# Local attention: turned queries and keys split in two parts for three-product scores

## The chip, the cores and the metric

The kernel runs on one core of one Trainium2 chip. The metric is the device time of one execution in microseconds (us). Every time below is from the kernel before. A core has five engines with queues of their own: PE (TensorE, matrix products and transposes), DVE (VectorE), ACT (ScalarE), POOL (GpSimd) and SP (which here only issues DMAs). They meet through semaphores alone.

## What is computed

The program computes `x + s * silu(g)`. Here `xn` is the layer norm of `x` (4 sequences of 1024 tokens, 256 wide), `s` is a causal attention over `xn` with 16 heads of 16, and `g` is a two-layer network over `xn` with local attention. The change touches only the local attention, which is, cut to what matters:

```python
for l in range(2):                                   # DEPTH
    q, k, v = split(shift_token(x) @ wqkv[l])        # 8 heads of 64
    q, k = l2norm(q) * q_scale, l2norm(k) * k_scale
    q, k = rotary_xpos(q, k)                         # q*cos*s + rotate_half(q)*sin*s ; k likewise with 1/s
    sim = einsum('bhwid,bhwjd->bhwij', 8 * q, [previous window of k, own window of k])   # windows of 128
    attn = softmax(mask(sim)); o = attn @ [previous v, own v]
    x = x + o @ wo[l]
    x = x + feed_forward(x)
```

## The kernel before

`program` runs five phases one after the other: `phase_project` (causal projections), `phase_causal`, then for each of two layers `phase_window` (local attention) and `phase_feed`, and last `phase_output`. Of them only `phase_window` is changed, so the change is met twice.

`phase_window` works through 32 tiles of 128 tokens; a tile is one window. Tile `w` runs through a software pipeline whose order is written out by hand in one `step` for each engine, called 32 times in a row. A step of tile `w` also does early parts of tiles `w+1` (`a1`), `w+2` (`a2`) and `w+3` (`a3`).

- PE, in a step: `project(w+2)` (18 products of 512 columns: the input in two fp32r parts times the weights in two parts, three products for each); `attend(w)`, that is `turn_p` (16 transposes of the probabilities), `turn_k(w+1)` and `turn_q(w+1)` (4 transposes each), and `values(w)` in four chunks; `turn_h(w+3)`; `score(w+1)` in two halves of four heads; `output(w)` (12 products of 256 columns).
- ACT: 8 `exps`, the copies `copy_q`, `copy_k`, `copy_v` of tile `w+2` out of PSUM, three `copy_p`, `copy_kt(w+1)`, `squares(w+2)`, `copy_qt(w+1)`, `copy_out(w)`, `turned(w+3)`.
- DVE: `normalise` of both halves, `unit(w+1)` (L997: turned values times inverse norms), `copy_last(w)` (L1021), `cosines(w+2)` (L984), `sum_squares(w+2)` (L991), `lo_out(w)` (L1025), `maxima` of the first half of `w+1` (L1007), `lo_of(w+3)` (L976), `maxima` of the second half, `residual(w)` (L1030).
- POOL: waits for both halves of `normalise(w)`, and then computes for tile `w+2` two `sines` (L826), the inverse norms (L832 and the power, L834, which wait for `sum_squares`), and `add` (L840), the sum of cosine and sine parts, which `unit` of the next step reads.

A head has 64 rows, so two heads lie in one 128-row block: `score` (L1181) makes for each of four blocks `c` two products, one on rows 0 to 63 and one on rows 64 to 127, and `score_place` puts them in different PSUM banks. Queries and keys are held as plain f32 (`qt`, `kt`; each score is one f32 product, which the trace shows as two records). The PSUM tile `pX` has four banks that several uses share: `turn_k` writes bank 1 and `turn_q` bank 3, and `turn_h(w+3)` and `project` write these banks again once the copies (`kt_copied`, `qt_copied`) have read them.

"Split" is used in this kernel for making a value v into hi = v rounded to fp32r and lo = v - hi (rounded again), so that a product of two values becomes hi*hi + hi*lo + lo*hi, three products of fp32r. Projections and `output` do this already: ACT writes the hi part, DVE subtracts for the lo part.

Of the kernel before, what the change touches and what calls it, by code (L numbers as in the profile page):

```python
# [731 lines left out]
def score_place(h):  # L732

    return 2 * (h // 4) + h % 2, h // 2 % 2


def phase_window(nc, K, W, F, layer, X, wqkv, wo, qk_scales, w1):

    NW = TILES
    (wo_st, wo_hi, wo_lo, scales, tab, xt, hs, thi, tlo, qk, sq, ss, ssc, rs,  # L740
     tc, tsn, rr, qkn, v, kt, qt, sm, nmax, sums, rsum, pe_, pn, pt, oth, otl, x1, pX, pS) = W.tensors
    qkv_st, qkv_hi, qkv_lo = W.weights
    base, masks = K.base, K.masks
    S = W.sems
# [22 lines left out]
    with nc.Block() as block:  # L767
# [51 lines left out]
        @block.gpsimd  # L819
        def _(pool):  # L820
            def rotated(w, j, it):

                pool.wait_ge(S["k_copied"], ONE + g0 + w + 1)
                pool.wait_ge(S["added"], ONE + g0 + w)
                for z in range(2):
                    pool.tensor_tensor(*sines(w, j, z), ALU.mult).then_inc(S["ts_ready"], 1)  # L826

            def inverse_norm(w, j, it):

                pool.wait_ge(S["ss_ready"], ONE + g0 + w + 1)  # L830
                pool.sem_inc(K.passed, 1)
                pool.tensor_scalar(ssc[:, :], ss[:, j % 2], 1e-24, None, ALU.max).then_inc(S["ssc_ready"], 1)  # L832
                pool.wait_ge(S["ssc_ready"], ONE + g0 + w + 1)
                pool.tensor_tensor(rs[:, j % 2], ssc[:, :], K.mhalf[:, :], ALU.pow).then_inc(S["rs_ready"], 1)  # L834

            def add(w, j, it):
                pool.wait_ge(S["tc_ready"], ONE + g0 + w + 1)
                pool.wait_ge(S["ts_ready"], ONE + 2 * (g0 + w) + 2)
                pool.wait_ge(S["qkn_ready"], ONE + g0 + w)
                pool.tensor_tensor(rr[:, :], tc[:, :], tsn[:, :], ALU.add).then_inc(S["added"], 1)  # L840

            def rope(nxt):
                if nxt:
                    rotated(*nxt)
                    inverse_norm(*nxt)
                    add(*nxt)


            pool.memset(kt[:, :, 1], 0.0).then_inc(S["cleared"], 1)
            pool.memset(v[:, 3], 0.0).then_inc(S["cleared"], 1)  # L850
            pool.wait_ge(S["w_loaded"], ONE + (layer + 1) * 2 * 16)
            pool.tensor_tensor(tab[:, :].rearrange("p t f d -> p t (f d)"), base[:, :].rearrange("p t f d -> p t (f d)"),
                               scales[:, :, :].rearrange("p f d -> p (f d)")[:, None, :]
                               .broadcast_to([P, TPB, 4 * LD]), ALU.mult).then_inc(S["tab_ready"], 1)
            pool.wait_ge(S["tab_ready"], ONE + layer + 1)
            inverse_norm(0, 0, 0)
            rope((1, 1, 0))

            pool.wait_ge(S["w_split"], ONE + 4 * layer + 4)
            pool.sem_inc(K.passed, 1)  # L860
            pool.memset(qkv_st[:, :, TAIL_COL:TAIL_COL + P], 0.0).then_inc(F.sems["cleared"], 1)

            def step(w, j, it):
                nxt = ahead(w, j, it, 2)
                if nxt:
                    pool.wait_ge(S["pn_ready"], ONE + 2 * (g0 + w) + 2)
                rope(nxt)

            steps(pool, step)

        @block.scalar
        def _(act):
# [50 lines left out]
                act.activation(qt[:, :, :], pX[:, 3].rearrange("p (c t) -> p c t", c=4), ACT.Copy)\  # L923
                   .then_inc(S["qt_copied"], 1)

            act.wait_ge(S["cleared"], ONE + 2 * layer + 2)
            turned(0, 0, 0)
            for z in range(3):
                act.wait_ge(S["qkv_loaded"][z], ONE + (layer + 1) * 16)
# [16 lines left out]
            def step(w, j, it):  # L946
                a1, a2, a3 = (ahead(w, j, it, n) for n in (1, 2, 3))
                exps(w, j, it, 0)
                exps(w, j, it, 1)
                if a2:  # L950
                    copy_q(*a2)
                    copy_k(*a2)
                    copy_v(*a2)
                for ch in range(3):
                    copy_p(w, j, it, ch)
                if a1:
                    copy_kt(*a1)
# [11 lines left out]
        def _(dve):  # L969
# [24 lines left out]
            def unit(w, j, it):  # L994
                dve.wait_ge(S["added"], ONE + g0 + w + 1)
                dve.wait_ge(S["rs_ready"], ONE + g0 + w + 1)
                dve.tensor_tensor(qkn[:, :].rearrange("p (h d) -> p h d", d=LD),  # L997
                                  rr[:, :].rearrange("p (h d) -> p h d", d=LD),
                                  rs[:, j % 2][:, :, None].broadcast_to([P, 2 * LH, LD]), ALU.mult)\
                   .then_inc(S["qkn_ready"], 1)  # L1000

            def maxima(w, t, hf):

# [41 lines left out]
            dve.tensor_tensor(rr[:, :], tc[:, :], tsn[:, :], ALU.add).then_inc(S["added"], 1)  # L1045
            split(3, wo_lo[:, :, :], wo_st[:, :, :], wo_hi[:, :, :])
            unit(0, 0, 0)
            cosines(1, 1, 0)
            sum_squares(1, 1, 0)
            maxima(0, 0, 0)  # L1050
# [3 lines left out]
            def step(w, j, it, t):  # L1054
# [2 lines left out]
                normalise(w, j, it, 1)  # L1057
                if a1:
                    unit(*a1)
                copy_last(w, j, it)  # L1060
                if a2:
                    cosines(*a2)
                    sum_squares(*a2)
                lo_out(w, j, it)
                if a1:
# [11 lines left out]
        def _(pe):  # L1077
            def turn_h(w, j, it):
                pe.wait_ge(S["x_loaded"][j], ONE + (layer * (NW // 4) + it + 1) * 32)
                pe.wait_ge(S["qt_copied"], ONE + g0 + w)  # L1080
                pe.wait_ge(S["t_lo"], ONE + g0 + w)
                pe.transpose(pX[:, 3, 0:P], xt[:, j, 0:P], K.ident[:, :])
                pe.transpose(pX[:, 3, P:D], hs[:, j], K.ident[:, :]).then_inc(S["t_ready"], 1)

            def project(w, j, it):
                pe.wait_ge(S["t_lo"], ONE + g0 + w + 1)
                for z in range(3):
                    if z == 0:
                        pe.wait_ge(S["kt_copied"], ONE + g0 + w)
                        pe.wait_ge(S["q_copied"], ONE + g0 + w)  # L1090
                    elif z == 1:
                        pe.wait_ge(S["ot_lo"], ONE + g0 + w)
                        pe.wait_ge(S["k_copied"], ONE + g0 + w)
                    else:
                        pe.wait_ge(S["qt_copied"], ONE + g0 + w)
                        pe.wait_ge(S["v_copied"], ONE + g0 + w)
                        if isinstance(w, int) and w == 0:
                            pe.wait_ge(S["t_lo"], ONE + g0 + 2)
# [32 lines left out]
            def attend(w, j, it):  # L1131
# [2 lines left out]
                pe.wait_ge(S["x1_ready"], ONE + 2 + g0 + w)  # L1134
                turn_p(w, j, it, 0, 0)
                pe.wait_ge(S["q_copied"], ONE + g0 + last)
                pe.wait_ge(S["kt_copied"], ONE + 1 + g0 + w + 1)
                turn_p(w, j, it, 1, 1)
                pe.wait_ge(S["v_copied"], ONE + g0 + last)
                pe.wait_ge(S["qt_copied"], ONE + 1 + g0 + w + 1)  # L1140
                turn_p(w, j, it, 2, 3)
                pe.wait_ge(S["pt_first"], ONE + 3 * (g0 + w) + 1)
                turn_p(w, j, it, 3, 0)
# [36 lines left out]

            def score(w, j, it, hf):  # L1181
                if hf == 0:
                    pe.wait_ge(S["kt_copied"], ONE + 1 + g0 + w + 1)
                    pe.wait_ge(S["qt_copied"], ONE + 1 + g0 + w + 1)
                if not isinstance(w, int) or w > 0:
                    pe.wait_ge(S["max_ready"], ONE + 2 * (g0 + w) + hf - 1)
                for c in (2 * hf, 2 * hf + 1):
                    for r in range(2):
                        rows = slice(r * LD, (r + 1) * LD)
                        bank, slot = score_place(2 * c + r)  # L1190
                        ins = pe.matmul(pS[:, bank, slot], qt[rows, c, :], kt[rows, c].rearrange("p s t -> p (s t)"),  # L1191
                                        start=True, stop=True)
                ins.then_inc(S["s_ready"], 1)

            for w in range(2):
                turn_h(w, w, 0)
            for w in range(2):
                project(w, w, 0)
            pe.wait_ge(S["cleared"], ONE + 2 * layer + 2)
            turn_k(0, 0, 0)  # L1200
            turn_q(0, 0, 0)
            score(0, 0, 0, 0)
# [522 lines left out]
def window_tensors(nc, c, W):  # L1725
# [8 lines left out]
        sb("ss", [P, 2, 2 * LH], F32), sb("ssc", [P, 2 * LH], F32), sb("rs", [P, 2, 2 * LH], F32),  # L1734
        sb("tc", [P, 2 * INNER], F32), sb("tsn", [P, 2 * INNER], F32), sb("rr", [P, 2 * INNER], F32),
        sb("qkn", [P, 2 * INNER], F32),
        sb("v", [P, 4, INNER], F32), sb("kt", [P, KI, 2, P], F32), sb("qt", [P, KI, P], F32),
        sb("sm", [P, LH, 2 * P], F32), sb("nmax", [P, LH], F32), sb("sums", [P, LH], F32), sb("rsum", [P, LH], F32),
        sb("pe", [P, LH, 2 * P], F32), sb("pn", [P, LH, 2 * P], F32), sb("pt", [P, 4, 512], F32),
        sb("oth", [P, INNER], F32R), sb("otl", [P, INNER], F32R), sb("x1", [P, 2, D], F32),  # L1740
# [19 lines left out]
def program(nc, x, wqk, wv, woc, wqkv, wo, qk_scales, ln_g, ln_b, w1, b1, w2, b2, tables, out):  # L1760

    with ExitStack() as c:
# [16 lines left out]
            "w_loaded", "w_hi", "w_split", "cleared", "tab_ready", "x1_ready", "ss_ready", "k_copied", "sq_ready",  # L1779
            "added", "ts_ready", "ssc_ready", "rs_ready", "rsum_ready", "pn_ready", "t_ready", "t_hi", "t_lo",  # L1780
            "q_ready", "k_ready", "v_ready", "q_copied", "v_copied", "max_ready", "exp_done", "pt_ready",
            "pt_first", "pt_last", "kt_ready", "kt_copied", "qt_ready", "qt_copied", "ot_ready", "ot_hi", "ot_lo",
            "tc_ready", "qkn_ready", "s_ready", "wo_ready"), {"qkv_loaded": 3, "x_loaded": 4, "x1_stored": 2})
        FS = semaphores(c, nc, "f_", (
            "w_loaded", "w1_loaded", "ln_loaded", "w_hi", "w_split", "cleared", "x2_ready", "hn_ready", "xb_ready", "mv_ready", "ve_ready",
# [2 lines left out]


        K.starts = [(x, ONE) for sems in (WS, FS) for v in sems.values() for x in (v if isinstance(v, list) else [v])]  # L1790
        K.starts += [(WS["kt_copied"], 1), (WS["exp_done"], 2), (WS["x1_ready"], 2), (WS["ot_lo"], 2),
                     (WS["qt_copied"], 1), (FS["act_ready"], 2), (FS["x2_ready"], 2)]
        made = c.enter_context(nc.semaphore("made"))
        K.zeroed = zeroed = c.enter_context(nc.semaphore("zeroed"))
        with nc.Block() as block:
# [86 lines left out]
```

## Time and profile before

| | |
|---|---|
| time, median of 3 runs | 2072.05 us (2068.73 to 2073.27) |
| the profiled execution, its own time | 2068.08 us |
| its span in the trace | 2066.3 us |
| PE busy | 1863.8 us (90%) |
| DVE busy | 1521.2 us (74%) |
| ACT busy | 1206.2 us (58%) |
| POOL busy | 955.0 us (46%) |
| PE in the score products, L1191 | 132.2 us summed durations, x1024 records, mean 398 ns with mutual overlap |

Busy is the time in which at least one of an engine's instructions runs. An instruction's record on DVE or ACT also covers its start-up and drain, so that the next record can begin some 0.08 us before it ends, and it covers time in which the instruction is held up after it began. Matmul records overlap much more; their pace is read from start to start.

### The profile page before, as it was taken

The page shows a single profiled execution, that of the slowest core. Times are in us where ns is not written, and L with a number is a line of the kernel's source. Part 1 is how long each engine was busy: PE and PEld are TensorE (multiplying, and loading weights), DVE is VectorE, ACT ScalarE, POOL GpSimd, SP SyncE. Part 2 cuts the span into 40 slices and gives each one's busy share as a digit, 9 for nine tenths or more (in the row PEclk, how much of TensorE's full clock was granted, in tenths as well). Part 3 has the DMA queues.
Part 4 walks back from the last instruction along what each step waited for, and adds up shares of the span by engine and source line. Part 5 has one row for each costly group of instructions (what it writes and reads, how often), then busy time and mean ns, then how long its engine had stood idle before and what let it go on. Part 6 is the DMA issues. An engine that isn't in the chain of part 4 may idle for free. (4 is left out here: it accounts for less than half of the span.)

```text
span 2066.3 us, 41715 instructions
## 1 busy us (share of the span) xinstructions
PE 1863.8 (90%) x12960; PEld 1337.3 (65%) x12960; DVE 1521.2 (74%) x4128; ACT 1206.2 (58%) x2501; POOL 955.0 (46%) x797
## 2 busy tenths in 40 slices
PE   5879999999996999999986999689999999699975
PEld 4733333333332788888875888578888887588875
DVE  5667888888872899999985554289999998555424
ACT  3414666666665677777774343267777777443323
POOL 3442122222222777777752333267777776233310
PEclk9868999999998999999998999899999999899988
DMA  5792456446512000000022221200000002211237
GB/s 199 240 185 39 63 75 81 63 65 83 70 21 67 14 26 26 27 27 26 26 66 61 57 58 49 80 14 26 26 26 26 26 26 66 64 34 58 62 119 242
DMA packets 150662, 134.67 MB, mean 65 GB/s; under 512 B 31298, under 2 KB 133118, under 8 KB 150398
## 3 DMA queue, kind: packets, MB, share of 16 engines
q1 hardware_dynamic: 149182, 131.75, 27.4%
q10 hardware_dynamic: 1344, 1.31, 0.2%
q8 instruction: 60, 0.98, 0.2%
q14 instruction: 76, 0.62, 0.1%
HBM read 86.60 MB, written 46.16 MB: 64 GB/s over the span
## 5 line engine op out<-in xcount | busy, mean ns | idle before, releaser
L636 ACT ACTIVATE ca_pr<-ca_pS 128x1024 f32<-128x1024 f32 (+3 forms) x384 | 296.5, 811 | 209.7 <-PE ca_pS L550 169.2
L895 ACT ACTIVATE w_pe<-w_sm,w_nmax 128x256 f32<-128x256 f32 x512 | 253.4, 497 | 140.7 <-DVE w_nmax L1007 140.7
L826 POOL TENSOR_TENSOR w_tsn<-w_qk,w_tab 128x512 f32<-128x512 f32 x124 | 251.0, 2045 | 163.0 <-DVE w_pn L1016 163.0
L470 POOL TENSOR_SCALAR_AFFINE_SELECT ca_pr<-ca_pr 128x256 f32<-128x256 f32 x256 | 103.8, 409 | 386.7 <-ACT ca_pr L636 382.2
L662 DVE CUSTOM_DVE_ANT_0 ca_masked<-ca_pR,ca_later 128x256 f32<-128x256 f32 (+3 forms) x512 | 235.6, 485 | 41.1 <-PE ca_pR L526 38.0
L526 PE MATMUL ca_pR<-ca_ks,ca_qs 96*128 96x512 bf16 (+3 forms) x768 | 220.3, 345 | 16.6 <-DVEq L719 13.2
L1007 DVE CUSTOM_DVE_ANT_0 w_sm<-w_pS,masks 128x256 f32<-128x256 f32 x512 | 185.7, 420 | 21.2 <-PE w_pS L1191 21.1
L666 DVE TENSOR_REDUCE ca_mx<-ca_pR 128x1 f32<-128x512 f32 x256 | 175.6, 686 | 29.0 <-PE ca_pR L526 27.2
L550 PE MATMUL ca_pS<-ca_qs,ca_ks 98*128 98x512 bf16 (+3 forms) x768 | 183.7, 330 | 8.7 <-issue 3.5
L834 POOL TENSOR_TENSOR w_rs<-w_ssc,mhalf 128x16 f32<-128x16 f32 x64 | 187.9, 2935 | 5.3
L1016 DVE TENSOR_SCALAR w_pn<-w_pe,w_rsum 128x256 f32<-128x256 f32 x512 | 186.9, 427 | 4.5
L526 PEld LDWEIGHTS ca_pR<-ca_ks,ca_qs 96*128 96x128 bf16 x768 | 70.5, 97 | 172.3 <-DVE ca_mx L662 89.6
L571 PE MATMUL ca_pO<-ca_pr,ca_va 128*32 128x512 f32 (+3 forms) x1536 | 164.2, 499 | 1.9 <-POOL ca_pr L470 1.1
L1104 PE MATMUL w_pX<-big_hi,w_thi 128*128 128x512 f32 x384 | 153.3, 399 | 9.8 <-DVE big_lo L972 9.8
L1327 POOL TENSOR_TENSOR f_alo<-f_af,f_ahi 128x512 fp32r<-128x512 f32 x80 | 105.7, 1326 | 116.9 <-ACT f_ahi L1379 116.9
L1104 PE MATMUL w_pX<-big_hi,w_tlo 128*128 128x512 f32 x384 | 151.9, 396 | 0.0
L1104 PE MATMUL w_pX<-big_lo,w_thi 128*128 128x512 f32 x384 | 151.7, 395 | 0.0
L1512 PE MATMUL f_pH<-f_thi,big_hi 128*128 128x512 f32 x352 | 142.9, 406 | 9.2 <-DVE f_tlo L1415 8.3
L840 POOL TENSOR_TENSOR w_rr<-w_tc,w_tsn 128x1024 f32<-128x1024 f32 x62 | 149.0, 2402 | 0.0
L1113 PE MATMUL w_pX<-ident,w_pn 128*128 128x128 f32 x1024 | 133.4, 280 | 15.2 <-DVE w_pn L1016 15.1
L1512 PE MATMUL f_pH<-f_tlo,big_hi 128*128 128x512 f32 x352 | 140.8, 400 | 0.0
L1512 PE MATMUL f_pH<-f_thi,big_lo 128*128 128x512 f32 x352 | 140.5, 399 | 0.0
(166 smaller groups left out, 4423.0 us busy)
## 6 DMA issues: line engine op xcount, KB each, us to landing
QKP<-p_parts SPq DMA_DIRECT2D x32, 384.0 KB, 2.9
ca_qs<-QKP SPq DMA_DIRECT2D x96, 128.0 KB, 6.8
ca_ks<-QKP SPq DMA_DIRECT2D x96, 128.0 KB, 7.2
w_xt<-X SPq DMA_DIRECT2D x64, 128.0 KB, 2.0
X<-w_x SPq DMA_DIRECT2D x64, 128.0 KB, 1.7
f_hh<-X SPq DMA_DIRECT2D x32, 256.0 KB, 4.9
f_xr<-X SPq DMA_DIRECT2D x16, 512.0 KB, 4.9
X<-f_x SPq DMA_DIRECT2D x16, 512.0 KB, 3.3
```

Of the source, the lines that this page charges most:

```text
L526: pe.matmul(bank[:, 0:w], qs[0:SHIFT_ROW, u, h, i * P:(i + 1) * P], ks[0:SHIFT_ROW, u, h, k0:k0 + w], start=True, stop=True).then_inc(ring ...
L550: ins = pe.matmul(pS[:, pair, hh, 0:w], ks[:, u, h, j * P:(j + 1) * P], qs[:, u, h, q0:q0 + w], start=True, stop=True)
L636: act.activation(pr[:, k % 2, pair, :, 0:w], pS[:, pair, :, 0:w], ACT.Exp, scale=CS).then_inc(p_ready, 1)
L662: dve.tensor_tensor_reduce(masked[:, jb % RING, 0:w], pR[jb % RING][:, 0:w], later[:, 512 - w:512], -1.0, BIG, ALU.add, ALU.min, mx[:, i, ...
L666: dve.tensor_reduce(mx[:, i, h, ch:ch + 1], pR[jb % RING][:, 0:w], AX.X, ALU.max, negate=True).then_inc(ring_free, 1)
L826: pool.tensor_tensor(*sines(w, j, z), ALU.mult).then_inc(S["ts_ready"], 1)
L834: pool.tensor_tensor(rs[:, j % 2], ssc[:, :], K.mhalf[:, :], ALU.pow).then_inc(S["rs_ready"], 1)
L895: ins = act.activation(pe_[:, h], sm[:, n], ACT.Exp, bias=nmax[:, n:n + 1], scale=-1.0, accum_out=sums[:, h:h + 1])
L1007: ins = dve.tensor_tensor_reduce(sm[:, n], pS[:, n // 2, n % 2], masks[:, 0 if t == 0 else 1 + t % 2], -1.0, BIG, ALU.add, ALU.min, nmax[: ...
L1016: ins = dve.tensor_scalar(pn[:, h], pe_[:, h], rsum[:, h:h + 1], None, ALU.mult)
L1104: ins = pe.matmul(pX[:, 1 + z], t[:, j % 2, k], m[:, k, cols], start=i == 0, stop=i == len(terms) - 1)
L1512: ins = pe.matmul(pH[:, ch % 2, half], m[:, k, cols], t[:, j, k], start=i == 0, stop=i == len(terms) - 1)
```

## The change

Turned queries and keys are now kept as fp32r hi parts (`qt`, `kt`) and lo parts (`qtl`, `ktl`). ACT's copies write the hi parts. Two new DVE instructions, `lo_k` and `lo_q`, make the lo parts out of the same PSUM banks. `score` makes three fp32r products for each head instead of one f32 product. The inverse norms are computed as before. On DVE the order of a step changes: `cosines(w+2)` comes ahead of `copy_last(w)`, and `lo_k(w+1)` and `lo_q(w+1)` stand between `copy_last(w)` and `sum_squares(w+2)`. On ACT `copy_qt(w+1)` comes ahead of `squares(w+2)`. On PE all waits for `kt_copied` and `qt_copied` become waits for `kt_lo` and `qt_lo`. POOL clears `ktl`'s first half too.

```diff
@@ pool, before the steps
-            pool.memset(kt[:, :, 1], 0.0).then_inc(S["cleared"], 1)
+            pool.memset(kt[:, :, 1].bitcast(F32), 0.0).then_inc(S["cleared"], 1)
+            pool.memset(ktl[:, :, 1].bitcast(F32), 0.0).then_inc(S["cleared"], 1)
@@ act step
                 if a1:
                     copy_kt(*a1)
+                    copy_qt(*a1)
                 if a2:
                     squares(*a2)
-                if a1:
-                    copy_qt(*a1)
@@ dve
+            def lo_k(w, j, it):
+                dve.wait_ge(S["kt_copied"], ONE + g0 + w + 1)
+                dve.tensor_tensor(ktl[:, :, j % 2], pX[:, 1].rearrange("p (c t) -> p c t", c=4),
+                                  kt[:, :, j % 2].bitcast(F32), ALU.subtract).then_inc(S["kt_lo"], 1)
+            def lo_q(w, j, it):
+                dve.wait_ge(S["qt_copied"], ONE + g0 + w + 1)
+                dve.tensor_tensor(qtl[:, :, :], pX[:, 3].rearrange("p (c t) -> p c t", c=4),
+                                  qt[:, :, :].bitcast(F32), ALU.subtract).then_inc(S["qt_lo"], 1)
@@ dve, before the steps
             unit(0, 0, 0)
+            lo_k(0, 0, 0)
+            lo_q(0, 0, 0)
             cosines(1, 1, 0)
@@ dve step
                 if a1:
                     unit(*a1)
-                copy_last(w, j, it)
                 if a2:
                     cosines(*a2)
+                copy_last(w, j, it)
+                if a1:
+                    lo_k(*a1)
+                    lo_q(*a1)
+                if a2:
                     sum_squares(*a2)
                 lo_out(w, j, it)
@@ pe, in turn_h, project, attend and score: each wait of this kind
-                pe.wait_ge(S["kt_copied"], ...)
-                pe.wait_ge(S["qt_copied"], ...)
+                pe.wait_ge(S["kt_lo"], ...)
+                pe.wait_ge(S["qt_lo"], ...)
@@ pe, score
                 for c in (2 * hf, 2 * hf + 1):
-                    for r in range(2):
-                        rows = slice(r * LD, (r + 1) * LD)
-                        bank, slot = score_place(2 * c + r)
-                        ins = pe.matmul(pS[:, bank, slot], qt[rows, c, :], kt[rows, c].rearrange("p s t -> p (s t)"),
-                                        start=True, stop=True)
+                    for i, (q, k) in enumerate(((qt, kt), (qt, ktl), (qtl, kt))):
+                        for r in range(2):
+                            rows = slice(r * LD, (r + 1) * LD)
+                            bank, slot = score_place(2 * c + r)
+                            ins = pe.matmul(pS[:, bank, slot], q[rows, c, :],
+                                            k[rows, c].rearrange("p s t -> p (s t)"), start=i == 0, stop=i == 2)
@@ window_tensors
-        sb("kt", [P, KI, 2, P], F32), sb("qt", [P, KI, P], F32),
+        sb("kt", [P, KI, 2, P], F32R), sb("ktl", [P, KI, 2, P], F32R),
+        sb("qt", [P, KI, P], F32R), sb("qtl", [P, KI, P], F32R),
```

## Rows read from the trace of the kernel before

**Rows 1.** Engines' busy time in a layer's window steps, in us.

```profile
core 0: us, PE busy (x) PEld busy (x) DVE busy (x) ACT busy (x) POOL busy (x), PEclk, DMA share, GB/s
683.00:1072.00 389.00, 384.70 (x3123) 323.66 (x3122) 358.60 (x1004) 299.28 (x819) 289.50 (x152) 1.00 0.10 31
```

**Rows 2.** Timeline of DVE: start us, us, instruction. `unit` of tiles 2 and 30.

```profile
700.93 1.22 DVE L997 TENSOR_TENSOR w_qkn<-w_rr,w_rs 128x1024 f32<-128x1024 f32 x1
...
1059.77 1.22 DVE L997 TENSOR_TENSOR w_qkn<-w_rr,w_rs 128x1024 f32<-128x1024 f32 x1
```

**Rows 3.** Timeline of PE in one period, merged where alike.

```profile
910.46 2.00 PE L1191 MATMUL w_pS<-w_kt,w_qt 64*128 64x256 f32 x16
912.38 0.39 PE L1177 MATMUL w_pX<-w_wo_hi,w_oth 128*128 128x256 f32 x1
912.61 0.28 PE L1177 MATMUL w_pX<-w_wo_lo,w_oth 128*128 128x256 f32 x1
912.73 0.28 PE L1177 MATMUL w_pX<-w_wo_hi,w_oth 128*128 128x256 f32 x1
```

**Rows 4.** Timeline of PE, window of 0.3 us at the first two score records.

```profile
910.46 0.49 PE L1191 MATMUL w_pS<-w_kt,w_qt 64*128 64x256 f32 x2
```

**Rows 5.** Timeline of DVE in the same period.

```profile
904.61 0.18 DVE L1013 RECIPROCAL w_rsum<-w_sums 128x4 f32<-128x4 f32 x1
...
905.88 1.22 DVE L997 TENSOR_TENSOR w_qkn<-w_rr,w_rs 128x1024 f32<-128x1024 f32 x1
907.32 0.69 DVE L1021 COPY w_pt<-w_pX 128x512 f32<-128x512 f32 x1 [0.22 <-PE w_pX L1113]
907.93 1.39 DVE L984 TENSOR_TENSOR w_tc<-w_qk,w_tab 128x1024 f32<-128x1024 f32 x1
909.44 1.22 DVE L991 TENSOR_REDUCE w_ss<-w_sq 128x16 f32<-128x1024 f32 x1
910.84 0.69 DVE L1025 TENSOR_TENSOR w_otl<-w_pX,w_oth 128x512 fp32r<-128x512 f32 x1 [0.17 <-ACT w_oth L905]
911.80 0.42 DVE L1007 CUSTOM_DVE_ANT_0 w_sm<-w_pS,masks 128x256 f32<-128x256 f32 x1 [0.27 <-PE w_pS L1191]
...
915.63 1.81 DVE L1016 TENSOR_SCALAR w_pn<-w_pe,w_rsum 128x256 f32<-128x256 f32 x4
917.38 0.18 DVE L1013 RECIPROCAL w_rsum<-w_sums 128x4 f32<-128x4 f32 x1
```

**Rows 6.** Timeline of POOL in the same period.

```profile
906.40 1.83 POOL L826 TENSOR_TENSOR w_tsn<-w_qk,w_tab 128x512 f32<-128x512 f32 x1 [2.67 <-DVE w_pn L1016]
908.20 2.29 POOL L826 TENSOR_TENSOR w_tsn<-w_qk,w_tab 128x512 f32<-128x512 f32 x1
910.86 0.25 POOL L832 TENSOR_SCALAR w_ssc<-w_ss 128x16 f32<-128x16 f32 x1 [0.38 <-DVE w_ss L991]
911.20 2.92 POOL L834 TENSOR_TENSOR w_rs<-w_ssc,mhalf 128x16 f32<-128x16 f32 x1
914.09 2.40 POOL L840 TENSOR_TENSOR w_rr<-w_tc,w_tsn 128x1024 f32<-128x1024 f32 x1
```

**Rows 7.** Timeline of ACT in the same period.

```profile
908.36 1.05 ACT L915 ACTIVATE w_sq<-w_qk 128x1024 f32<-128x1024 f32 x1
909.30 0.59 ACT L923 ACTIVATE w_qt<-w_pX 128x512 f32<-128x512 f32 x1
...
913.30 0.51 ACT L895 ACTIVATE w_pe<-w_sm,w_nmax 128x256 f32<-128x256 f32 x1 [2.22 <-DVE w_nmax L1007]
...
917.25 0.58 ACT L884 ACTIVATE w_qk<-w_pX 128x512 f32<-128x512 f32 x1
```

**Rows 8.** Timeline of DVE at the start of layer 1's window phase.

```profile
672.31 2.21 DVE L997 TENSOR_TENSOR w_qkn<-w_rr,w_rs 128x1024 f32<-128x1024 f32 x1 [0.49 <-POOL w_rs L834]
674.44 2.30 DVE L984 TENSOR_TENSOR w_tc<-w_qk,w_tab 128x1024 f32<-128x1024 f32 x1
```

**Rows 9.** Timeline of POOL at the same place.

```profile
672.18 1.26 POOL L826 TENSOR_TENSOR w_tsn<-w_qk,w_tab 128x512 f32<-128x512 f32 x1
673.40 2.26 POOL L826 TENSOR_TENSOR w_tsn<-w_qk,w_tab 128x512 f32<-128x512 f32 x1
```

More of the change, by code:

```diff
@@ L740, in phase_window @@
     (wo_st, wo_hi, wo_lo, scales, tab, xt, hs, thi, tlo, qk, sq, ss, ssc, rs,
-     tc, tsn, rr, qkn, v, kt, qt, sm, nmax, sums, rsum, pe_, pn, pt, oth, otl, x1, pX, pS) = W.tensors
+     tc, tsn, rr, qkn, v, kt, ktl, qt, qtl, sm, nmax, sums, rsum, pe_, pn, pt, oth, otl, x1, pX, pS) = W.tensors
     qkv_st, qkv_hi, qkv_lo = W.weights
@@ L924, in copy_qt @@
                    .then_inc(S["qt_copied"], 1)
-            act.wait_ge(S["cleared"], ONE + 2 * layer + 2)
+            act.wait_ge(S["cleared"], ONE + 3 * layer + 3)
             turned(0, 0, 0)
@@ L1079, in turn_h @@
                 pe.wait_ge(S["x_loaded"][j], ONE + (layer * (NW // 4) + it + 1) * 32)
-                pe.wait_ge(S["qt_copied"], ONE + g0 + w)
+                pe.wait_ge(S["qt_lo"], ONE + g0 + w)
                 pe.wait_ge(S["t_lo"], ONE + g0 + w)
@@ L1088, in project @@
                     if z == 0:
-                        pe.wait_ge(S["kt_copied"], ONE + g0 + w)
+                        pe.wait_ge(S["kt_lo"], ONE + g0 + w)
                         pe.wait_ge(S["q_copied"], ONE + g0 + w)
@@ L1094, in project @@
                     else:
-                        pe.wait_ge(S["qt_copied"], ONE + g0 + w)
+                        pe.wait_ge(S["qt_lo"], ONE + g0 + w)
                         pe.wait_ge(S["v_copied"], ONE + g0 + w)
@@ L1136, in attend @@
                 pe.wait_ge(S["q_copied"], ONE + g0 + last)
-                pe.wait_ge(S["kt_copied"], ONE + 1 + g0 + w + 1)
+                pe.wait_ge(S["kt_lo"], ONE + 1 + g0 + w + 1)
                 turn_p(w, j, it, 1, 1)
                 pe.wait_ge(S["v_copied"], ONE + g0 + last)
-                pe.wait_ge(S["qt_copied"], ONE + 1 + g0 + w + 1)
+                pe.wait_ge(S["qt_lo"], ONE + 1 + g0 + w + 1)
                 turn_p(w, j, it, 2, 3)
@@ L1182, in score @@
                 if hf == 0:
-                    pe.wait_ge(S["kt_copied"], ONE + 1 + g0 + w + 1)
-                    pe.wait_ge(S["qt_copied"], ONE + 1 + g0 + w + 1)
+                    pe.wait_ge(S["kt_lo"], ONE + 1 + g0 + w + 1)
+                    pe.wait_ge(S["qt_lo"], ONE + 1 + g0 + w + 1)
                 if not isinstance(w, int) or w > 0:
@@ L1198, in _ @@
                 project(w, w, 0)
-            pe.wait_ge(S["cleared"], ONE + 2 * layer + 2)
+            pe.wait_ge(S["cleared"], ONE + 3 * layer + 3)
             turn_k(0, 0, 0)
@@ L1736, in window_tensors @@
         sb("qkn", [P, 2 * INNER], F32),
-        sb("v", [P, 4, INNER], F32), sb("kt", [P, KI, 2, P], F32), sb("qt", [P, KI, P], F32),
+        sb("v", [P, 4, INNER], F32), sb("kt", [P, KI, 2, P], F32R), sb("ktl", [P, KI, 2, P], F32R),
+        sb("qt", [P, KI, P], F32R), sb("qtl", [P, KI, P], F32R),
         sb("sm", [P, LH, 2 * P], F32), sb("nmax", [P, LH], F32), sb("sums", [P, LH], F32), sb("rsum", [P, LH], F32),
@@ L1781, in program @@
             "q_ready", "k_ready", "v_ready", "q_copied", "v_copied", "max_ready", "exp_done", "pt_ready",
-            "pt_first", "pt_last", "kt_ready", "kt_copied", "qt_ready", "qt_copied", "ot_ready", "ot_hi", "ot_lo",
+            "pt_first", "pt_last", "kt_ready", "kt_copied", "kt_lo", "qt_ready", "qt_copied", "qt_lo", "ot_ready", "ot_hi", "ot_lo",
             "tc_ready", "qkn_ready", "s_ready", "wo_ready"), {"qkv_loaded": 3, "x_loaded": 4, "x1_stored": 2})
@@ L1790, in program @@
         K.starts = [(x, ONE) for sems in (WS, FS) for v in sems.values() for x in (v if isinstance(v, list) else [v])]
-        K.starts += [(WS["kt_copied"], 1), (WS["exp_done"], 2), (WS["x1_ready"], 2), (WS["ot_lo"], 2),
-                     (WS["qt_copied"], 1), (FS["act_ready"], 2), (FS["x2_ready"], 2)]
+        K.starts += [(WS["kt_lo"], 1), (WS["exp_done"], 2), (WS["x1_ready"], 2), (WS["ot_lo"], 2),
+                     (WS["qt_lo"], 1), (FS["act_ready"], 2), (FS["x2_ready"], 2)]
         made = c.enter_context(nc.semaphore("made"))
```

## The prediction

> **What bounds the kernel now.** The changed code runs only in the window phases, so I read those alone: first the busy time by stretch, then one period engine by engine.
>
> The stretch view [rows 1] shows PE busy for 384.7 of 389 us at full granted clock, DVE for 358.6, ACT 299.3, POOL 289.5. PE looks like the bound, and DVE is not far off. One tile takes one period: from a reciprocal to the same one a tile later is 917.38 - 904.61 = 12.77 us [rows 5]. Over 28 tiles, `unit` to `unit`, it is (1059.77 - 700.93) / 28 = 12.82 [rows 2]; some steps have a little loop overhead.
>
> A busy share does not show loops, and there is one that passes through POOL and DVE. I follow it in [rows 5, 6]:
> - `sum_squares` ends at 910.66 (909.44 + 1.22). POOL starts L832 at 910.86, the power at 911.20, `add` at 914.09, and ends it at 916.49.
> - DVE's first normalising group (L1016) began at 915.63 and takes 1.81 for four, while 905.88 - 904.61 is only 1.27 for a reciprocal and four of them. It sat blocked until POOL's `add` let go, and the next reciprocal is at 917.38.
> - Reciprocal to `unit` is 1.27. `unit` runs 1.22.
> - POOL's first `sines` is recorded from 906.40 but takes 1.83 and ends at 908.23, and the second 2.29. An undisturbed one took 1.26 [rows 9]. The first waited for `unit` to end (907.10), the second for `cosines`.
> - `cosines` starts at 907.93, at once behind `copy_last`, and takes 1.39 against 1.22 for `unit`, which is as large: it waits for the first `sines` and ends at 909.32. `sum_squares` follows at 909.44.
>
> Along this loop there is 0.20 us between `sum_squares` and L832, a hand-over, and 0.12 ahead of `sum_squares`; nothing else is free. It closes in 12.77 by itself. So the kernel has two bounds of nearly one length: PE's order, and this loop. In the present order `copy_last` costs the loop nothing, because it lies in the time in which POOL's first `sines` holds the port.
>
> **The change part by part, per tile.**
>
> Scores on PE. Now they take 912.38 - 910.46 = 1.92, for 8 f32 products, 16 records [rows 3]. The two row halves run side by side: two records that last together 0.49, with a mean of 398 ns for one on this line [rows 4]. The new form has 24 fp32r products of 256 columns. The nearest row is `output`, fp32r with 256 columns, one per 0.12 (912.73 - 912.61) [rows 3]. If halves still run side by side that is 12 x 0.12 = 1.44 and some ramp, a gain of 0.3 to 0.48. If they don't, it is 24 x 0.12 = 2.88, a loss of 0.96, and PE's order takes 13.73. I take the first, since the same halves do it in f32; as the sum turns out, even the second stays under the new loop.
>
> The Trainium skill (TensorE: Matmul & The Clock Gate, section LDWEIGHTS) prices a weight load by its columns, however few rows: about 107 ns for 128. As an estimate from that page, 24 loads in series would be 2.57 us, more than today's scores. The trace has no fp32r load on half the rows; for f32 it shows both halves going together.
>
> DVE's two subtractions. They read PSUM and SBUF and write 128x512 fp32r, exactly the form of `lo_out`, 0.69 [rows 5]. Such an instruction advances the queue by 0.61 (`copy_last` to `cosines`, 907.93 - 907.32). So 1.22 more DVE work per tile, in front of `sum_squares`, that is inside the loop.
>
> `cosines` moved ahead of `copy_last`. This takes `copy_last` out of its cover. The question is who gets the port when `unit` ends: POOL's `sines`, pending since 906.40, or `cosines`, next in DVE's queue. The start of the phase has just that order, `unit` then `cosines` with `sines` pending: `cosines` is recorded 674.44 with 2.30, nearly twice its length, and the pending `sines` 673.40 with 2.26, ending 675.66 [rows 8, 9]. `unit` ended 674.52; `sines` took the next 1.14, `cosines` only then. POOL won. So in the new step `cosines` still ends at 909.32, as before, and `copy_last` comes behind it.
>
> Then, in this period's time: `copy_last` 909.24, `lo_k` 909.85, `lo_q` 910.46, `sum_squares` 911.07 instead of 909.44: 1.63 later (0.61 x 3 - 0.20 for waits that go). The rest of the loop is unchanged: L832, the power and `add` follow `sum_squares` at fixed distance, and the next reciprocal follows `add`. The period becomes 12.77 + 1.63 = 14.40.
>
> Does anything end later still? `score` now waits for `lo_q`, done at 911.15, against a start of 910.46 now. `turn_h` (0.4) comes between, so scores start at some 911.6 and the first half is ready near 912.7; `maxima` follows `lo_out`, which ends 912.9, so it starts at 912.8 instead of 911.80 [rows 5]. The exponentials start 1.5 later and fill 3.95 (913.30 to 917.25) [rows 7], which ends them at 918.3; the reciprocal of the second half is due at 904.61 + 14.40 = 919.0. Hidden by 0.7. With serial scores `maxima` would start 0.7 later, and it just ties. PE stops before `values`' last chunk for `copy_last` (about 0.4) and before `turn_h` for `lo_q`; its work of 12.3 to 13.7 fits in 14.40. If the loop were not the cover, these waits would cost up to 1.
>
> ACT's exchange (`copy_qt` before `squares`): squares end near 909.92 instead of 909.41 (908.36 + 1.05) [rows 7], hidden behind 911.07. The added memset is some 0.5 us while loads are on their way: nothing, 0.5 per layer at most.
>
> The sum. From 12.82 to 14.40 is 1.58 a tile. 31 steps in each of two layers have a next tile: 62 x 1.58 = 98 us. First and last tiles have other orders (`cosines(1)` waits for the two subtractions; the last two steps have no `cosines`); I leave them at the same price, give or take 6. On the profiled execution's 2068.08 (span 2066.3 and 1.8 around it) this gives 2166. The median of the runs shown is 4 above that execution, 0.2%, which is also about what a measurement can tell from no change; half of it added, the forecast is 2168 us. Its own range is 2150 to 2185.
>
> The Trainium skill (SBUF — State Buffer, section SBUF: two separate sides) says that VectorE and GpSimd share a port pair as an exclusive lock, taken by an instruction with two SBUF inputs too, held by whichever starts first while the other fully blocks. The rows of `unit`, `cosines` and `sines` agree (2.30 against 1.22). It does not say who is next when both wait; read as VectorE going straight on, it would give rival A.
>
> **The rivals.**
>
> A: VectorE keeps the port. `cosines` runs 907.02 to 908.24, `copy_last` and the low parts follow, and `sum_squares` then waits for ACT's squares at 909.97 or so, 0.53 later than now. Period 13.30, 62 x 0.48 = 30, about 2100. For it: the two are back to back in one queue. Against: both rows at the phase's start. 13%.
>
> B: faster. The loop is no bound, and PE's order remains one; the subtractions lie in DVE's idle 30 us, and PE's gain of 0.3 to 0.48 is paid out 62 times, about 25 us: 2047. It decides in my favour or not at `sum_squares`: the loop would need 1.63 of slack, and I find 0.12. 7%.
>
> C: the fp32r products on half the rows neither pair nor have weights loaded ahead. The step after a cold load is 0.23 (912.61 - 912.38) [rows 3]; 24 x 0.23 = 5.5, PE's order 16.4, +3.6 a tile, about 2290. Against: f32 pairs. 5%.
>
> D: the change makes no difference, since waits that go pay for the subtractions: about 2072, 3%.
>
> **How the numbers follow.** The main case has 72%. The likeliest time is 2168. The range goes from 2092 (it takes in A) to 2190 (the main case with serial scores and dear edges, or a few stretches at the lower clock now that PE idles some 1.5 us a tile); B, C, D and half of the spill are left out. Faster by over 0.2%: 8%. Within 0.2%: 3%. Slower: 89%.
>
> **What would show it.** Right: a period near 14.4 in the distance between two L997; `cosines` records near 2.3 and following `unit` at once; the power starting some 1.6 later behind `unit`; PE idle over a us a tile, waiting for DVE; score products in pairs, 12 steps of 0.12. `cosines` at 1.22 means A. A period under 12.8 with PE still full means B. Score steps of 0.2 or more mean C. The forecast is wrong if the power or `add` starts at another distance from `sum_squares` than now.

## The result and the profile after

The changed kernel takes 2098.14 us (median of 4 runs, 2095.24 to 2101.14), against 2071.68 us for the kernel before beside it. The ratio is 1.013, 95% interval 1.0109 to 1.015. It is slower, as forecast, but by 26 us and not by 96: this is the time of rival A. It lies inside the forecast's wide range (2092 to 2190) only because that range took rival A in; the main case's own range was 2150 to 2185.

The period first: DVE's timeline, `unit` of tiles 2 and 30, answering [rows 2].

```profile
702.93 1.22 DVE L997 TENSOR_TENSOR w_qkn<-w_rr,w_rs 128x1024 f32<-128x1024 f32 x1
...
1073.14 1.22 DVE L997 TENSOR_TENSOR w_qkn<-w_rr,w_rs 128x1024 f32<-128x1024 f32 x1
```

(1073.14 - 702.93) / 28 = 13.22 us, against 12.82. Over 62 tiles that is 25 us, nearly all of the difference. The first step of each layer is 1.3 longer and the second 0.3 to 0.6 shorter; from `unit` of tile 0 to `unit` of tile 31 both layers together take 25.3 us more. The granted clock is 1.00 from 690 to 1060, as in [rows 1], so the clock has no part in it.

One period of DVE, answering [rows 5] (the score maxima are left out):

```profile
913.22 0.16 DVE L1023 RECIPROCAL w_rsum<-w_sums 128x4 f32<-128x4 f32 x1
...
914.47 1.22 DVE L997 TENSOR_TENSOR w_qkn<-w_rr,w_rs 128x1024 f32<-128x1024 f32 x1
915.61 1.22 DVE L984 TENSOR_TENSOR w_tc<-w_qk,w_tab 128x1024 f32<-128x1024 f32 x1
916.74 0.68 DVE L1031 COPY w_pt<-w_pX 128x512 f32<-128x512 f32 x1
917.34 0.68 DVE L1004 TENSOR_TENSOR w_ktl<-w_pX,w_kt 128x512 fp32r<-128x512 f32 x1
917.94 0.68 DVE L1009 TENSOR_TENSOR w_qtl<-w_pX,w_qt 128x512 fp32r<-128x512 f32 x1
918.54 1.21 DVE L991 TENSOR_REDUCE w_ss<-w_sq 128x16 f32<-128x1024 f32 x1
...
924.08 2.44 DVE L1026 TENSOR_SCALAR w_pn<-w_pe,w_rsum 128x256 f32<-128x256 f32 x4
926.43 0.17 DVE L1023 RECIPROCAL w_rsum<-w_sums 128x4 f32<-128x4 f32 x1
```

The second row from `unit` decides the case. `cosines` (L984) follows at once and takes 1.22, where the forecast had 2.3; so it is in all 60 steady tiles (1 to 30 of each layer). The two low parts stand behind it, and `sum_squares` (L991) starts 5.32 behind the reciprocal. In [rows 5] it was 4.83, so it is 0.49 later; forecast was 1.63.

POOL's timeline of the same period, answering [rows 6]:

```profile
915.00 4.24 POOL L826 TENSOR_TENSOR w_tsn<-w_qk,w_tab 128x512 f32<-128x512 f32 x2 [2.64 <-DVE w_pn L1026]
919.94 0.25 POOL L832 TENSOR_SCALAR w_ssc<-w_ss 128x16 f32<-128x16 f32 x1 [0.71 <-DVE w_ss L991]
920.28 2.92 POOL L834 TENSOR_TENSOR w_rs<-w_ssc,mhalf 128x16 f32<-128x16 f32 x1
923.17 2.39 POOL L840 TENSOR_TENSOR w_rr<-w_tc,w_tsn 128x1024 f32<-128x1024 f32 x1
```

The record covers both `sines` and the wait of the first one for both of VectorE's instructions. L832, the power and `add` follow `sum_squares` at the same distances as before, within 0.02. `add` ends at 925.56, the held-up L1026 (2.44 for four, now) is over just before 926.43, and the period closes: 926.43 - 913.22 = 13.21.

ACT in that period, answering [rows 7]:

```profile
916.45 0.60 ACT L910 ACTIVATE w_kt<-w_pX 128x512 fp32r<-128x512 f32 x1 [0.55 <-PE w_pX L1175]
916.95 0.59 ACT L924 ACTIVATE w_qt<-w_pX 128x512 fp32r<-128x512 f32 x1
917.42 1.06 ACT L916 ACTIVATE w_sq<-w_qk 128x1024 f32<-128x1024 f32 x1
...
925.71 0.58 ACT L885 ACTIVATE w_qk<-w_pX 128x512 f32<-128x512 f32 x1
```

`squares` ends at 918.48, when `sum_squares` starts at 918.54. Two chains reach that start within 0.1 us: VectorE's queue, and ScalarE's `squares` in its new place behind `copy_qt`. And the exponentials end at 925.8, 0.6 before the reciprocal could use them.

PE in the scores, answering [rows 3, 4]:

```profile
919.06 0.39 PE L1208 MATMUL w_pS<-w_kt,w_qt 64*128 64x256 f32 x2
919.28 0.28 PE L1208 MATMUL w_pS<-w_ktl,w_qt 64*128 64x256 f32 x2
919.40 0.29 PE L1208 MATMUL w_pS<-w_kt,w_qtl 64*128 64x256 f32 x2
...
920.69 0.39 PE L1193 MATMUL w_pX<-w_wo_hi,w_oth 128*128 128x256 f32 x1
```

The halves go in pairs, one pair per 0.12, and the scores take 1.63 instead of 1.92. TensorE gained the 0.3 a tile and gives it back by waiting. Its busy share hardly tells this (361.23 of 370 us between 690 and 1060, against 384.7 of 389 in [rows 1]), but its waits do. Its weight loads for the transposes of the probabilities wait for `normalise` (us in total, times, longest, between 700 and 1000), first in the kernel before and then in the changed one:

```profile
PEld w_pX L1113 <- DVE w_pn L1016: 0.7, 2, 0.4
PEld w_pX L1129 <- DVE w_pn L1026: 20.6, 46, 0.5
```

### The profile page after: what moved, and what is told of

It is laid out like the page before. It is cut to its first block and busy times, and to the rows that moved or that the text cites. A ratio compares the mean times of both kernels' runs of the same rounds, so it can differ in the third digit from the quotient of the medians.

```text
span 2098.4 us, 42871 instructions
## 1 busy us (share of the span) xinstructions
PE 1873.4 (89%) x13472; PEld 1339.3 (64%) x13472; DVE 1600.5 (76%) x4256; ACT 1217.0 (58%) x2501; POOL 967.3 (46%) x799
## 5 line engine op out<-in xcount | busy, mean ns | idle before, releaser
L826 POOL TENSOR_TENSOR w_tsn<-w_qk,w_tab 128x512 f32<-128x512 f32 x124 | 262.5, 2137 | 157.6 <-DVE w_pn L1026 157.6
L1026 DVE TENSOR_SCALAR w_pn<-w_pe,w_rsum 128x256 f32<-128x256 f32 x512 | 227.6, 506 | 4.5
L1129 PE MATMUL w_pX<-ident,w_pn 128*128 128x128 f32 x1024 | 144.0, 285 | 30.4 <-DVE w_pn L1026 26.0
L1129 PEld LDWEIGHTS w_pX<-ident,w_pn 128*128 128x128 f32 x1024 | 113.6, 144 | 70.9 <-DVE w_pn L1026 70.7
```

The costliest lines, as they stand in the source:

```text
L1026: ins = dve.tensor_scalar(pn[:, h], pe_[:, h], rsum[:, h:h + 1], None, ALU.mult)
L1129: ins = pe.transpose(pX[:, bank, o:o + P], pn[:, 2 * ch + hh, s * P:(s + 1) * P], K.ident[:, :])
```

## The experiments

All times are medians, and each ratio is to the kernel before on the same chip. The theory after the result: the loop through `sum_squares`, power, `add` and `normalise` sets the period; VectorE keeps the port, so that `cosines` runs ahead of the pending `sines`; and `sum_squares` has two legs in front of it, VectorE's own queue and ScalarE's `squares`. Each diff is cut to the lines that matter, and `...` marks what is left out.

**Taking the subtractions away.**

```diff
-                    lo_k(*a1)
-                    lo_q(*a1)
...
-                    for i, (q, k) in enumerate(((qt, kt), (qt, ktl), (qtl, kt))):
+                    for i, (q, k) in enumerate(((qt, kt), (qt, kt), (qt, kt))):
...
```

> The changed kernel without VectorE's two subtractions for the low parts; the three products read the high parts alone, so the low parts are left out of the scores. Theory (loop with two legs): the period of 13.22 is the POOL/VectorE loop, and it is set where sum_squares starts, 5.32 us behind the reciprocal; two things end there together, VectorE's queue (cosines, copy_last, lo_k, lo_q) and ScalarE's squares, which now stand behind copy_qt and end 5.27 behind the reciprocal. Taking the subtractions away then changes little: period 13.15 to 13.25, time 2093 to 2100 us. Rival (subtractions alone): the two times 0.6 us are the cost; sum_squares then starts at 4.83 or earlier as before, period 12.6 to 12.8, time 2055 to 2072 us.

Measured: 2096.86 us, ratio 1.0118 (1.0101 to 1.0135). 1.2 us of VectorE's work a tile is gone (TensorE waits for the copies instead) and the time stays. DVE's timeline shows who holds `sum_squares` now:

```profile
904.48 0.68 DVE L1031 COPY w_pt<-w_pX 128x512 f32<-128x512 f32 x1
906.23 1.22 DVE L991 TENSOR_REDUCE w_ss<-w_sq 128x16 f32<-128x1024 f32 x1 [1.07 <-ACT w_sq L916]
```

**The same, with ScalarE's old order.**

```diff
                     copy_kt(*a1)
-                    copy_qt(*a1)
                 if a2:
                     squares(*a2)
+                if a1:
+                    copy_qt(*a1)
```

> As the run without the subtractions (low parts left out of the scores), and ScalarE's order as before: squares ahead of copy_qt. Theory (two legs): squares end 4.80 behind the reciprocal again, so sum_squares starts 0.49 earlier; the loop gives 12.73 and TensorE's order about 12.5; period 12.7, time about 2068 us (2062 to 2074). Rival (subtractions alone): the same time as the run without them and ScalarE's new order.

Measured: 2067.08 us, ratio 0.9978 (0.9968 to 0.9988), period 12.74. `sum_squares` starts 3.57 behind `unit`, against 4.05 in the run above: as the theory had it, ScalarE's exchange alone costs the full amount (2096.86 against 2067.08). The run also gives the loop's own length, 12.74, a little under TensorE's 12.8; that is why `sum_squares` 0.49 later made the period only 0.40 longer.

**The changed kernel with ScalarE's old order** (the same exchange, with the low parts left in).

```diff
-                    copy_qt(*a1)
                 if a2:
                     squares(*a2)
+                if a1:
+                    copy_qt(*a1)
```

> The changed kernel with ScalarE's squares ahead of copy_qt again. Theory (two legs): squares end 3.53 behind unit, but copy_qt ends only at 4.02, so lo_q waits for it and sum_squares follows at 4.7 instead of 4.07: period 13.83, time 2136 us (2128 to 2142). Rival (ScalarE's leg alone costs the 0.4 a tile): 2070 us.

Measured: 2134.5 us, ratio 1.0294 (1.0276 to 1.0313), period 13.81. DVE's timeline has the wait where it was expected:

```profile
914.91 0.68 DVE L1005 TENSOR_TENSOR w_ktl<-w_pX,w_kt 128x512 fp32r<-128x512 f32 x1
916.07 0.69 DVE L1010 TENSOR_TENSOR w_qtl<-w_pX,w_qt 128x512 fp32r<-128x512 f32 x1 [0.48 <-ACT w_qt L924]
916.68 1.21 DVE L992 TENSOR_REDUCE w_ss<-w_sq 128x16 f32<-128x1024 f32 x1
```

So the exchange on ScalarE serves the low parts: with them it saves 36 us, without them it costs 30.

**`lo_q` made twice.**

```diff
+                dve.tensor_tensor(qtx[:, w % 2], pX[:, 3].rearrange("p (c t) -> p c t", c=4),
+                                  qt[:, :, :].bitcast(F32), ALU.subtract)
                 dve.tensor_tensor(qtl[:, :, :], pX[:, 3]...
```

> The changed kernel with lo_q's subtraction made twice (the first result goes to a spare tile). Theory: VectorE's queue is one of the two legs, so sum_squares starts 0.60 later, period 13.8, time 2135 us (2128 to 2140). Rival (only ScalarE's squares set it, and VectorE has room): under 2105 us.

Measured: 2140.61 us, ratio 1.0337 (1.0321 to 1.0353), period 13.82. One more subtraction on VectorE costs its full 0.60 a tile and taking two away saves nothing; that is what two legs of one length look like.

**f32 scores in the changed kernel.**

```diff
-                    for i, (q, k) in enumerate(((qt, kt), (qt, ktl), (qtl, kt))):
-                        for r in range(2):
...
+                    for r in range(2):
...
+                        ins = pe.matmul(pS[:, bank, slot], qt[rows, c, :].bitcast(F32),
+                                        kt[rows, c].rearrange("p s t -> p (s t)").bitcast(F32), start=True, stop=True)
```

> The changed kernel with one f32 product for each head instead of three fp32r ones (it reads the high parts alone, the low parts are made and not used). Theory: TensorE is not the bound, it has 0.7 us a tile to spare; scores take 1.92 instead of 1.63 a tile and nothing is late: 2094 to 2102 us. Rival (TensorE with its new waits sets the period): 0.29 a tile more, 62 times, 2116 us.

Measured: 2099.24 us, ratio 1.0133 (1.0114 to 1.0152), period 13.22. The faster scores are worth nothing where they stand.

**`copy_last` ahead of `cosines` again.**

```diff
+                copy_last(w, j, it)
                 if a2:
                     cosines(*a2)
-                copy_last(w, j, it)
```

> The changed kernel with copy_last ahead of cosines again on VectorE; all else as changed. Theory (the port goes to who asked first): GpSimd's sines ask during unit, while VectorE's next user of the port is behind copy_last; sines gets the port, cosines is recorded at 1.3 to 1.5 us and ends 2.3 us behind unit's end; the two subtractions then stand behind it, sum_squares 0.55 later, period about 13.77, time about 2132 us (2122 to 2140). Rival (ScalarE's squares bound the loop, VectorE's order has room): same as changed, 2098.

Measured: 2128.74 us, ratio 1.0278 (1.0261 to 1.0296), period 13.72. In DVE's timeline `cosines` is held up again:

```profile
911.08 1.22 DVE L997 TENSOR_TENSOR w_qkn<-w_rr,w_rs 128x1024 f32<-128x1024 f32 x1
912.35 0.69 DVE L1031 COPY w_pt<-w_pX 128x512 f32<-128x512 f32 x1
912.96 1.57 DVE L984 TENSOR_TENSOR w_tc<-w_qk,w_tab 128x1024 f32<-128x1024 f32 x1
```

**The exchange alone, in the kernel before.**

```diff
-                copy_last(w, j, it)
                 if a2:
                     cosines(*a2)
+                copy_last(w, j, it)
+                if a2:
                     sum_squares(*a2)
```

> The kernel before with cosines ahead of copy_last and nothing else. Theory: VectorE keeps the port, cosines is recorded at 1.22 and ends 1.1 us earlier; sum_squares still waits for ScalarE's squares and TensorE's order still sets the period: 2067 to 2075 us. Rival (sines gets the port between unit and cosines, as forecast): copy_last 1.3 later, values wait for it, 2085 us or more.

Measured: 2071.37 us, ratio 0.9988 (0.9978 to 0.9999), period 12.83. DVE's timeline:

```profile
906.60 1.22 DVE L997 TENSOR_TENSOR w_qkn<-w_rr,w_rs 128x1024 f32<-128x1024 f32 x1
907.73 1.22 DVE L984 TENSOR_TENSOR w_tc<-w_qk,w_tab 128x1024 f32<-128x1024 f32 x1
908.87 0.69 DVE L1021 COPY w_pt<-w_pX 128x512 f32<-128x512 f32 x1
910.16 1.22 DVE L991 TENSOR_REDUCE w_ss<-w_sq 128x16 f32<-128x1024 f32 x1 [0.61 <-ACT w_sq L915]
```

`cosines` ends over 1 us earlier, and `squares` holds `sum_squares` where it was. Alone the exchange does nothing; beside the low parts it is worth 30 us (2128.74 against 2098.14).

**`unit` made late,** to bring back the meeting of [rows 8, 9] in every tile.

```diff
                 normalise(w, j, it, 1)
+                dve.tensor_reduce(dum[:, w % 2:w % 2 + 1], masks[:, 0:2].rearrange("p m s -> p (m s)"), AX.X, ALU.add)
                 if a1:
                     unit(*a1)
```

> The changed kernel with an idle reduction (128x512 of a constant, result unused) on VectorE ahead of unit, which makes unit start 0.61 later, behind GpSimd's first sines. Then unit and the second sines ask at the same time when the first sines ends, and cosines asks behind them. Theory (the port goes to who asked first, and VectorE's next instruction asks when the one ahead of it really begins): the second sines gets in between; cosines recorded at 2.2 to 2.4 us, unit at 1.9 to 2.5; sum_squares 2.9 later, period near 16.1, time near 2275 us. Rival (VectorE keeps the port for the next instruction in its queue): cosines recorded at 1.22, sum_squares 1.7 later, period near 14.95, time near 2205 us.

Measured: 2184.02 us (2 runs, 2174.63 and 2193.4), ratio 1.0545 (1.05 to 1.0589). Neither time came, since the meeting fell on the edge. In the trace of the first run `unit` still got the port first in most tiles, and the period was 13.82 (the reduction's 0.60 and nothing else). In 15 tiles of the steady part, and in 4 at the phases' ends, `sines` got it first, and there the period was 16.0 (15.7 to 15.8 at the ends). First a tile of the one kind, on DVE:

```profile
950.93 1.22 DVE L997 TENSOR_TENSOR w_qkn<-w_rr,w_rs 128x1024 f32<-128x1024 f32 x1
952.06 1.22 DVE L984 TENSOR_TENSOR w_tc<-w_qk,w_tab 128x1024 f32<-128x1024 f32 x1
```

and on POOL, whose instruction is recorded as long as its wait:

```profile
950.86 3.58 POOL L826 TENSOR_TENSOR w_tsn<-w_qk,w_tab 128x512 f32<-128x512 f32 x1 [2.64 <-DVE w_pn L1026]
```

Then a tile of the other kind, on DVE:

```profile
934.93 2.30 DVE L997 TENSOR_TENSOR w_qkn<-w_rr,w_rs 128x1024 f32<-128x1024 f32 x1
937.16 2.31 DVE L984 TENSOR_TENSOR w_tc<-w_qk,w_tab 128x1024 f32<-128x1024 f32 x1
```

and POOL's two:

```profile
934.86 1.29 POOL L826 TENSOR_TENSOR w_tsn<-w_qk,w_tab 128x512 f32<-128x512 f32 x1 [2.64 <-DVE w_pn L1026]
936.11 2.27 POOL L826 TENSOR_TENSOR w_tsn<-w_qk,w_tab 128x512 f32<-128x512 f32 x1
```

All steady tiles are of one of these kinds. Where `unit` (L997) got the port without waiting, `cosines` had it after it; where `unit` itself had waited, POOL's second `sines` came between. The rival's case, `unit` held up and `cosines` not, with a period of 14.95, did not occur once. The expected 16.1 is met for the tiles of the second kind (16.0); that most tiles would not be of that kind was not foreseen. Who asked first cannot be read from these rows. `sines` is recorded as starting ahead of `unit` in both kinds, by 0.03 to 0.074 us in the first and by 0.073 to 0.079 in the second (0.28 at the phases' ends).

**The power replaced by a multiply** (norms left out).

```diff
-                pool.tensor_tensor(rs[:, j % 2], ssc[:, :], K.mhalf[:, :], ALU.pow)...
+                pool.tensor_tensor(rs[:, j % 2], ssc[:, :], K.mhalf[:, :], ALU.mult)...
```

> The changed kernel with GpSimd's power replaced by a multiply, so that the norms are left out; about 2.6 us less in the loop. Theory (POOL/VectorE loop is the bound): add no longer holds up normalise; next are the exponentials, which end 11.33 behind unit, then period 12.62, time 2058 to 2066 us. Rival (VectorE's or TensorE's own work is the bound at 13.2): unchanged, 2098.

Measured: 2063.6 us, ratio 0.9963 (0.9951 to 0.9975), period 12.66. The reciprocal of the second half now waits for the exponentials, and no longer for a held-up `normalise`:

```profile
913.68 0.18 DVE L1023 RECIPROCAL w_rsum<-w_sums 128x4 f32<-128x4 f32 x1
915.65 0.18 DVE L1023 RECIPROCAL w_rsum<-w_sums 128x4 f32<-128x4 f32 x1 [0.61 <-ACT w_pe L896]
```

**`squares` early,** a failed attempt at a faster version.

```diff
@@ act step
                     copy_k(*a2)
+                    squares(*a2)
                     copy_v(*a2)
-                for ch in range(3):
+                for ch in range(4):
                     copy_p(w, j, it, ch)
...
-                    squares(*a2)
@@ dve step
                     cosines(*a2)
-                copy_last(w, j, it)
+                    sum_squares(*a2)
                 if a1:
                     lo_k(*a1)
                     lo_q(*a1)
-                if a2:
-                    sum_squares(*a2)
@@ pe step
+                if a1:
+                    score(*a1, 0)
                 if a3:
                     turn_h(*a3)
                 if a1:
-                    score(*a1, 0)
                     score(*a1, 1)
```

> The changed kernel reordered so that neither leg stands in front of sum_squares: ScalarE makes squares right behind copy_k and takes over copy_last; VectorE's order is unit, cosines, sum_squares, lo_k, lo_q; TensorE puts turn_h between the two halves of score. Theory: the power starts some 0.7 earlier than in the changed kernel, the loop allows 12.5; copy_qt and with it scores come 0.5 later, and the exponentials set a period of 12.7 to 12.8: 2064 to 2074 us. Rival (the split costs VectorE 1.2 us a tile wherever it stands): 2090 us or more.

Measured: 2111.73 us, ratio 1.0194 (1.018 to 1.0208), period 13.48. The power does start 0.74 earlier behind `unit`, but I had not followed PE: it stands still for `copy_v`, which `squares` had put off, ahead of the transposes, values and scores. On ACT:

```profile
908.01 1.06 ACT L917 ACTIVATE w_sq<-w_qk 128x1024 f32<-128x1024 f32 x1
908.97 0.58 ACT L921 ACTIVATE w_v<-w_pX 128x512 f32<-128x512 f32 x1
```

and on PE, which waits for it:

```profile
909.68 1.09 PE L1127 MATMUL w_pX<-ident,w_pn 128*128 128x128 f32 x8 [0.70 <-ACT w_v L921]
```

**`add` ahead of the inverse norms,** in the changed kernel.

```diff
                     rotated(*nxt)
-                    inverse_norm(*nxt)
                     add(*nxt)
+                    inverse_norm(*nxt)
```

> The changed kernel with GpSimd's add ahead of the inverse norms instead of behind them. It needs only the sines and cosines, so it should run from 4.7 to 7.1 behind unit and no longer hold up normalise; the power ends near 10.5, well before the next unit needs it. Theory (the loop sumsquares - power - add - normalise was the bound of the changed kernel): the exponentials are next, period 12.62 as with the cheap power, 2060 to 2067 us, faster than both kernels. Rival (the power itself, now near the normalising, holds it up as add did): the power ends 0.65 earlier than add did, period 12.6 to 13.0, up to 2085.

Measured: 2063.82 us (2061.59 to 2066.13), ratio 0.9947 (0.9934 to 0.996), period 12.67. One line moved, and the kernel is faster than the kernel before and the changed one, with the whole computation in it. DVE:

```profile
913.99 1.14 DVE L1026 TENSOR_SCALAR w_pn<-w_pe,w_rsum 128x256 f32<-128x256 f32 x4
915.75 0.18 DVE L1023 RECIPROCAL w_rsum<-w_sums 128x4 f32<-128x4 f32 x1 [0.62 <-ACT w_pe L896]
```

and POOL:

```profile
909.22 2.40 POOL L840 TENSOR_TENSOR w_rr<-w_tc,w_tsn 128x1024 f32<-128x1024 f32 x1
911.59 0.25 POOL L832 TENSOR_SCALAR w_ssc<-w_ss 128x16 f32<-128x16 f32 x1
911.92 3.00 POOL L834 TENSOR_TENSOR w_rs<-w_ssc,mhalf 128x16 f32<-128x16 f32 x1
```

`add` is over at 911.62. The power runs until 914.92, over the normalising of 913.99, which takes its plain 1.14.

**The same in the kernel before.**

```diff
                     rotated(*nxt)
-                    inverse_norm(*nxt)
                     add(*nxt)
+                    inverse_norm(*nxt)
```

> The kernel before with GpSimd's add ahead of the inverse norms. Theory (two bounds of one length, and TensorE's order is one of them): the period stays at 12.75 to 12.82, time within 0.3% of 2071 us. Rival (the loop alone was the bound of the kernel before): period under 12.6, 2058 us or less.

Measured: 2072.15 us, ratio 0.9987 (0.9976 to 0.9998), period 12.83. Nothing gained: with the loop gone TensorE's order still takes 12.8. Its weight loads wait for `normalise` 0.3 us in all between 700 and 1060, and VectorE's maxima wait for its scores in every tile (us in total, times, longest), as they do not in the run above:

```profile
DVE w_sm L1007 <- PE w_pS L1191: 7.9, 28, 0.6
```

With `add` moved in both kernels, the split one is the faster by 8 us (2063.82 against 2072.15), period 12.67 against 12.83. That fits TensorE's order being shorter there by its scores; no run separates this.

## Why the prediction was wrong

- **The bounds before: right.** TensorE's order (12.83 in the run with `add` moved) and the loop (12.74 in the run without low parts and with ScalarE's old order) are both near 12.8. Moving `add` alone gained nothing in the kernel before and 34 us in the changed one.
- **The loop as the bound after: right.** The cheap power and the moved `add` each take it away, and the two runs land at 2063.6 and 2063.82. In both the reciprocal then waits 0.6 us for the exponentials.
- **Scores: right.** Pairs, 0.12 each, 0.29 gained per tile and hidden; f32 scores cost nothing. (The 132.2 us in the table ahead of the forecast is the scores' busy time, not summed durations.)
- **The price of a low part: right.** 0.60 each, against 0.61.
- **The failing step:** "POOL won. So in the new step `cosines` still ends at 909.32, as before, and `copy_last` comes behind it." In the changed kernel VectorE won, in each of the 60 steady tiles: `cosines` took 1.22 instead of 2.3 and ended 1.1 us earlier than this step had it. So of the 1.63 us by which `sum_squares` was to start later, 1.63 - 0.49 = 1.14 did not come. Over 62 tiles that is the 70 us between forecast and result.
- **Why the row misled.** [rows 8, 9] show a meeting with another history. There `unit` itself had waited (2.21 instead of 1.22) for a `sines` that ran, and the second `sines` was asking when the first let go. In the steady step `unit` had the port at once. I took the outcome of one meeting as a rule for who wins, without asking what had gone before it. The forecast's rival A was this case, with a period of 13.30 and 2100 us; it had the mechanism and got 13%.
- **ScalarE's exchange: half right.** `squares` near 909.92 was worked out and called hidden. With VectorE's leg shorter it became the second leg of equal length, worth the same 0.49. In the kernel before it was already `squares` (ends at 909.41) that released `sum_squares` at 909.44, and not `cosines`: in the exchange alone `cosines` ended 1.1 earlier and `sum_squares` stayed at 3.56 behind `unit`.
- **The exponentials: hidden, as forecast, but its sum has a slip.** It says that they start 1.5 later; the 1.0 later of its own maxima is what gives its 918.3. In the changed kernel the maxima start 7.04 behind the reciprocal instead of 7.19, so the exponentials came earlier and not later.

What stays open is the chip's rule behind it. The late `unit` fits an order of asking in which VectorE's next instruction asks when the one ahead of it gets the port. It fits as well a rule that passes the port on after a wait and not otherwise, but such a rule would have to be VectorE's alone. In [rows 8, 9], and in each tile of the second kind of the late `unit`, POOL's first `sines` had the port without waiting (1.26 and 1.29 us), and `unit` had it next, not the second `sines`. No tile parts the two rules for VectorE.

## What to carry to other kernels

A busy share does not tell the bound: TensorE was busy for 98 to 99% of the steady part under either bound here. Look for a loop that passes through several engines and write down its links with their starts; two bounds of one length show as a change that costs in full one way and gains nothing the other. A blocked instruction hides what stands in its shadow, so before moving it find out who will be asking for the same resource and who asked first, and take a precedent from the trace only if the instruction ahead of it began in the same way. If an engine's long instruction holds up another engine, first try whether it can run at another time: here one moved line was worth more than the faster products.

## What the hardware showed beside this

- Engines meet at a shared port too, and not through semaphores alone. VectorE's `unit` and `cosines`, with two SBUF inputs, were held up by POOL's `sines` of 512 columns (recorded at up to 2.31 us instead of 1.22) and held it up in turn: it was recorded at up to 3.58 us, for 1.26 of work. VectorE's SBUF-to-SBUF `normalise` was held up by POOL's `add` over 1024 columns (2.44 for four instead of 1.14).
- POOL's power over 16 columns, 3.00 us long, did not hold up VectorE's normalising that ran inside it (1.14 for four, as undisturbed), while `add`, 2.40 long, did.
- fp32r products with 64 rows run in pairs on the two halves of the array like f32 ones: 0.12 us for two of 256 columns.
- One kernel can switch from tile to tile between two periods, 13.82 and 16.0 us, where the starts of the two engines' records differ by less than 0.01 us between the two kinds of tile.
